# Where the softmax shift is split into two bf16 parts: in VectorE after the maxima, or behind TensorE's transpose

## The reference

```python
x = x + L0_attn(layernorm(x))                    # 16 heads of width 8, 4 key/value heads
x = x + L0_xattn(layernorm(x), ctx, ctx)         # 16 heads of width 8
x = x + L0_ffn(layernorm(x))                     # 8 experts, 2 chosen, 1 shared
x = x + L1_attn(layernorm(x))                    # shared heads, relative bias
x = x + L1_xattn(layernorm(x), ctx, ctx, mask)   # 16 heads of width 8
x = x + L1_ffn(layernorm(x))

# the attention of the two 16-head forms, for each batch and head
scores = Q @ K.T / sqrt(8)
attn = softmax(scores)          # exp(scores - max) / sum
out = attn @ V
```

## Time and profile before

| | |
|---|---|
| time, median of 3 runs | 1096.98 us (1094.63 to 1103.36) |
| profiled execution, its span from first to last instruction | 1087.7 us |
| the median less that span | 9.3 us |
| busy share of the span: PE, PEld, DVE, ACT, POOL | 89%, 64%, 79%, 64%, 60% |
| chain that ended last | PE 61%, DVE 19%, issue 8%, DMA 5%, ACT 3%, POOL 3% |
| steps of the stage heads | about 31 to 355 us of the span |
| steps of the stage cross1 | about 736 to 920 us |

### The profile page before, as it was taken

The page is one execution under the profiler, slowest core; times in us unless marked ns, Lnnn a source line. Parts: engine busy times, 40 slices in busy tenths (PEclk is TensorE's granted clock), DMA queues, the critical chain, the costliest instruction groups (busy, mean ns, idle before and its releaser), DMA issues.

```text
span 1087.7 us, 33962 instructions
## 1 busy us (share of the span) xinstructions
PE 973.1 (89%) x10494; PEld 694.1 (64%) x10494; DVE 855.0 (79%) x2398; ACT 692.1 (64%) x1801; POOL 649.3 (60%) x1020
## 2 busy tenths in 40 slices
PE   3699999989998888999998889889999999768997
PEld 2466666656665667777776677665656655556885
DVE  6588899888888778888887888776787877657665
ACT  1377777777776743555665887673666666546775
POOL 8757778877676466640675786168667752323443
PEclk9599999999998979999998999998999999989999
DMA  5776567985666201332332111035555640054551
GB/s 147 181 148 132 116 139 163 185 162 134 143 153 171 74 34 50 98 105 77 106 104 55 37 31 38 26 64 133 115 113 129 130 106 18 6 196 167 194 193 29
DMA packets 81460, 119.69 MB, mean 110 GB/s; under 512 B 16720, under 2 KB 62704, under 8 KB 80288
## 3 DMA queue, kind: packets, MB, share of 16 engines
q1 hardware_dynamic: 66704, 85.24, 32.9%
q0 software_dynamic: 9472, 27.27, 8.2%
q10 hardware_dynamic: 5136, 5.31, 2.5%
HBM read 80.75 MB, written 36.18 MB: 107 GB/s over the span
## 4 chain that ended last, share of the span: by engine, by line
PE 61%; DVE 19%; issue 8%; DMA 5%; ACT 3%; POOL 3%; SPq 1%; DVEq 0%; POOLq 0%; ACTq 0%
PE heads_ps_pv L992 4%; PE heads_ps_max L970 4%; DVE heads_neg_max L770 4%; PE cross_ps_max L960 4%; PE experts_ps_gu L2488 4%; PE cross_ps_max L970 3%; PE cross_ps_pv L992 3%; DMA QK<-heads_qk_parts 2%; PE experts_ps_gu L2490 2%; PE experts_ps_gu L2489 2%; PE heads_ps_out L1054 2%; PE experts_ps_y L2509 2%; PE experts_ps_y L2510 2%; PE experts_ps_hT L2496 1%; PE cross_ps_qk L1316 1%
## 5 line engine op out<-in xcount | busy, mean ns | idle before, releaser
L770 DVE TENSOR_REDUCE heads_neg_max<-heads_ps_max 128x4 f32<-128x512 f32 x256 | 169.5, 681 | 36.0 <-PE heads_ps_max L970 34.4
L844 ACT ACTIVATE heads_E<-heads_ps_exp 128x512 f32<-128x512 f32 x256 | 150.1, 603 | 22.1 <-PE heads_ps_pv L992 17.3
L970 PE MATMUL heads_ps_max<-QK 48*128 48x128 bf16 x1024 | 102.9, 226 | 10.2 <-DMA QK<-heads_qk_parts 5.8
L770 DVE TENSOR_REDUCE cross_neg_max<-cross_ps_max 128x4 f32<-128x512 f32 x128 | 86.2, 682 | 29.5 <-PE cross_ps_max L970 28.9
L974 PE MATMUL heads_ps_exp<-QK 50*128 50x128 bf16 x1024 | 103.0, 222 | 0.0
L2182 POOL DMA_INDIRECT experts_gathered<-experts_y_dram,experts_index x64 | 62.0, 969 | 65.4 <-DMA experts_y_dram<-experts_y_sb 44.1
L844 ACT ACTIVATE cross_E<-cross_ps_exp 128x512 f32<-128x512 f32 x128 | 76.5, 599 | 33.1 <-PE cross_ps_exp L974 17.0
L2404 ACT ACTIVATE experts_act_out<-experts_ps_gu 128x256 f32<-128x256 f32 x110 | 42.3, 384 | 83.0 <-PE experts_ps_gu L2490 82.9
L970 PEld LDWEIGHTS heads_ps_max<-QK 48*128 48x128 bf16 x1024 | 58.9, 97 | 52.2 <-issue 21.0
L1613 POOL TENSOR_TENSOR experts_hidden_lo<-experts_hidden,experts_hidden_hi 128x512 fp32r<-128x512 f32 x32 | 41.4, 1293 | 73.9 <-ACT experts_hidden_hi L1837 66.8
L992 PE MATMUL heads_ps_pv<-heads_E,heads_V 128*32 128x128 f32 x2048 | 84.8, 285 | 0.0
(11 more groups left out here) (325 smaller groups left out, 3173.3 us busy)
## 6 DMA issues: line engine op xcount, KB each, us to landing
experts_share<-experts_cT_dram SPq DMA_DIRECT2D x7, 2304.0 KB, 8.8
heads_qk_parts<-heads_parts POOLq DMA_DIRECT2D x32, 384.0 KB, 4.7
QK<-heads_qk_parts SPq DMA_DIRECT2D x64, 192.0 KB
QK<-heads_qk_parts SPq DMA_DIRECT2D x64, 128.0 KB
cross_qk_parts<-cross_parts POOLq DMA_DIRECT2D x16, 384.0 KB, 4.2
QK<-cross_qk_parts SPq DMA_DIRECT2D x32, 192.0 KB
experts_xs_dram<-load_stats SPq DMA_DIRECT2D x26, 192.0 KB, 3.0
experts_xs<-experts_xs_dram SPq DMA_DIRECT2D x78, 64.0 KB
```

What stands on the lines that cost most here:

```text
L770: nc.vector.tensor_reduce(neg_max[:, half, heads.start:heads.stop], ps_max[:, u % 2, :].rearrange("q (h k) -> q h k", h=HU), AX.X, ALU.max ...
L844: nc.scalar.activation(E[:, half, heads.start:heads.stop, :], ps_exp[:, u % 2, :].rearrange("k (h q) -> k h q", h=HU), ACT.Exp, scale=scal ...
L970: last_max = nc.tensor.matmul(ps_max[:, u % 2, i * S:(i + 1) * S], QK[q_of][rows, 0, h, max_of], QK[q_of][rows, 1, h, max_of], start=not m ...
```

## The change

VectorE no longer makes `shift` after the fourth maximum. TensorE transposes the 16 columns of fp32 negative maxima (now in two buffers) into 16 fp32 rows of PSUM, as soon as the fourth maximum is taken. ScalarE's copy from PSUM, still L856's place, writes the high part in bf16; a new VectorE subtraction (`shift_low`, behind the output's addition L784 and ahead of the third maximum) takes PSUM less the high part and writes the low part. It, no longer the copy, raises `shiftT_ready`, for which SyncE (ahead of L606), `project_qk` and the next `turn_shift` wait. SyncE's two DMAs now take one part each for both halves, instead of both parts of one half each; each still moves 16 rows of 128 bf16. The second set of semaphores (`shift_ready`) goes.

```diff
@@ -446,9 +446,8 @@
         rest = sb("rest", [D, GT])
         parts = [sb(f"parts{p}", [D, 2, PARTS, GT], BF16) for p in range(2)]
         V = [sb(f"V{p}", [S, G, H * TILE + SLOT]) for p in range(RING)]
-        neg_max = sb("neg_max", [S, HALVES, HH])
-        shift = sb("shift", [S, HALVES, SHIFT, HH], BF16)
-        shiftT = [sb(f"shiftT{p}", [SHIFT * H, S], BF16) for p in range(2)]
+        neg_max = [sb(f"neg_max{p}", [S, HALVES, HH]) for p in range(2)]
+        shiftT = [sb(f"shiftT{p}", [H, SHIFT, S], BF16) for p in range(2)]
         E = sb("E", [S, HALVES, HH, S])
         recip = sb("recip", [S, H])
         oT_spread = sb("oT_spread", [D, 2, S])
@@ -456,7 +455,7 @@
         oT = sb("oT", [D, S])
         qk_dram = [nc.dram_tensor(f"{name}_qk_parts{p}", (2, PARTS, D, GT), BF16) for p in range(RING)]
 
-        ps_shiftT = ps_qk[0:SHIFT * H, 0, 0:S // 2].bitcast(BF16)
+        ps_shiftT = ps_qk[0:H, 0, 0:S]
         o_spread = ps_pv[:, 0:2 * S].rearrange("q (h d) -> q h d", d=SLOT)
 
         masked = mask is not None
@@ -492,7 +491,6 @@
         max_scored = sem("max_scored")
         max_taken = sem("max_taken")
         shift_hi = sem("shift_hi")
-        shift_ready = sem("shift_ready")
         shiftT_made = sem("shiftT_made")
         shiftT_ready = sem("shiftT_ready")
         shift_placed = [sem(f"shift_placed{p}") for p in range(2)]
@@ -601,9 +599,9 @@
                     turned = shiftT[(t.k + MA - 1) % 2]
                     sp.wait_ge(shiftT_ready, t.batch(1, MA))
                     apart(sp, t, turns_sp)
-                    for half in range(HALVES):
-                        at = half * BASE + ROWS
-                        sp.dma_start(QK[p][at:at + SHIFT, 0, :, j * S:j * S + S], turned[half * SHIFT * HH:(half + 1) * SHIFT * HH, :]).then_inc(shift_placed[(t.k + MA - 1) % 2], 16)
+                    for i in range(SHIFT):
+                        at = ROWS + i
+                        sp.dma_start(QK[p][at:at + BASE + 1:BASE, 0, :, j * S:j * S + S], turned[:, i, :]).then_inc(shift_placed[(t.k + MA - 1) % 2], 16)
                 if t.has(-2 * LA, 2 * NG_ALL - 1 - 2 * LA):
 
                     p, half = slot(t, LA), t.k % 2
@@ -765,10 +763,17 @@
                 if t.has(-MA, NB_ALL - MA - 1):
                     dve.wait_ge(max_scored, t.batch(UNITS, MA * UNITS + u + 1))
                     if u == 0:
-                        need(dve, shift_ready, t.batch(1, MA))
+                        need(dve, shiftT_made, t.batch(1, MA - 1))
                     half, heads = heads_of(u)
-                    nc.vector.tensor_reduce(neg_max[:, half, heads.start:heads.stop], ps_max[:, u % 2, :].rearrange("q (h k) -> q h k", h=HU),
+                    nc.vector.tensor_reduce(neg_max[(t.k + MA) % 2][:, half, heads.start:heads.stop], ps_max[:, u % 2, :].rearrange("q (h k) -> q h k", h=HU),
                                             AX.X, ALU.max, negate=True).then_inc(max_taken, 1)
+
+            def shift_low(t):
+
+                if t.has(1 - MA, NB_ALL - MA):
+                    turned = shiftT[(t.k + MA - 1) % 2]
+                    dve.wait_ge(shift_hi, t.batch(1, MA))
+                    nc.vector.tensor_tensor(turned[:, 1, :], ps_shiftT, turned[:, 0, :], ALU.subtract).then_inc(shiftT_ready, 1)
 
             def emit(t):
                 odd = t.k % 2 == 1
@@ -782,6 +787,7 @@
                     dve.wait_ge(x_biased, t.group(1, 0))
                     xb = row(x_sb, t.batch(1, -2 - layer_at(t, -2) * B))
                     nc.vector.tensor_tensor(xb, ps_out[:, 1, :], xb, ALU.add).then_inc(x_done, 1)
+                shift_low(t)
                 maxima(t, 2)
                 if t.has(1, NB_ALL):
 
@@ -791,13 +797,6 @@
                     need(dve, oT_made, t.batch(1, -1))
                     nc.vector.tensor_tensor(o_tok[:], o_spread[:, :, 0:HD], recip[:].unsqueeze(2).to_broadcast([S, H, HD]), ALU.mult).then_inc(o_ready, 1)
                 maxima(t, 3)
-                if t.has(-MA, NB_ALL - MA - 1):
-
-                    dve.wait_ge(max_taken, t.batch(UNITS, (MA + 1) * UNITS))
-                    need(dve, shiftT_made, t.batch(1, MA))
-                    nc.vector.tensor_copy(shift[:, :, 0, :], neg_max[:]).then_inc(shift_hi, 1)
-                    dve.wait_ge(shift_hi, t.batch(1, MA + 1))
-                    nc.vector.tensor_tensor(shift[:, :, 1, :], neg_max[:], shift[:, :, 0, :], ALU.subtract).then_inc(shift_ready, 1)
                 if t.has(2, NB_ALL + 1):
                     dve.wait_ge(x_done, t.batch(1, -1))
                     apart(dve, t, turns_dve)
@@ -853,7 +852,7 @@
                     q = (t.k + MA - 1) % 2
                     act.wait_ge(shiftT_made, t.batch(1, MA))
                     need(act, shift_placed[q], t.group(32, 32))
-                    nc.scalar.copy(shiftT[q][:], ps_shiftT).then_inc(shiftT_ready, 1)
+                    nc.scalar.copy(shiftT[q][:, 0, :], ps_shiftT).then_inc(shift_hi, 1)
                 if prev:
                     act.wait_ge(pv_done, t.batch(UNITS, 0))
                     need(act, spread_turned, t.batch(1, -1))
@@ -1028,11 +1027,11 @@
 
             def turn_shift(t):
 
-                pe.wait_ge(shift_ready, t.batch(1, MA))
+                pe.wait_ge(max_taken, t.batch(UNITS, MA * UNITS))
                 need(pe, shiftT_ready, t.batch(1, MA - 1))
                 qk = t.group(2, 2 * FA)
                 need(pe, qk_ready, min(2 * NG_ALL, qk) if t.reg is None else qk)
-                nc.tensor.transpose(ps_shiftT, shift[:].rearrange("q a i h -> q (a i h)"), identb[:]).then_inc(shiftT_made, 1)
+                nc.tensor.transpose(ps_shiftT, neg_max[(t.k + MA - 1) % 2][:].rearrange("q a h -> q (a h)"), ident[:]).then_inc(shiftT_made, 1)
 
             def turn_spread(t):
```

## The result

The kernel after took 1114.84 us (median of 4 executions, 1108.13 to 1124.21) against 1095.81 of before beside it: a ratio of 1.0178, 95% interval 1.0127 to 1.0229. The sign and the mechanism of the prediction held; the size did not, as the loss is about 19 to 28 us and not 9.5: the first set lies near the upper end of the range on record (1089 to 1117 us), the second above it. The profiled execution was the slowest of the first four, with a span of 1122.3 us; that of before had 1087.7. The profiles of e4_before_held and e7_bf16_maxima were taken in disturbed executions, so of these only the lists of waits, stretches at full clock and, once, the place of a fall of the clock are read.

A forecast was written before the change was run, and what follows sets the result against it. It took the SyncE loop, with the QK loads queued behind the later shift, to bind heads after the change: +8.5 us there, +1.0 in cross1, +9.5 on 1096.98, so 1106.5 us, range 1089 to 1117.

The forecast's parts named there:

- L1035's wait goes: In heads, `turn_shift` no longer waits for VectorE's L800; these waits were counted as 32.8 us in 62.
- the second rival: The engines win: the compute loop decides in heads, 1085 us; chance 0.12.
- The shift is ready 1.3 us later than the copy: Odd steps of heads: shift ready at about +3.15, L606 at +3.2, first L621 at +4.5 us.
- shift later still: Rival: ScalarE's casts or VectorE's order hold the subtraction 0.4 us more, +11 on top, 1117 us; chance 0.14.
- The subtraction costs 0.29 us: New VectorE subtraction takes 0.29 us like L784, bounds 0.17 and 0.74, never stretched by GpSimd.
- The landing: Heads, first L621 to the half's landing: 5.8 us to 161 us, 6.0 to 201, 7.5 to 233, 5.3 to 323.
- The 0.05 us from the landing to the scores: SyncE loop in heads: 0.05 us added to the period between the QK load's landing and the scores.
- The estimate of 2.3 us: Skill page's landing time for a 128 KB DMA; set aside for the trace's 4.0 to 4.7 us on SyncE's queue.
- Half of the third stretch: Heads, 201 to 233 us: 3 pairs x 1.35 = +4.1 us, of which half was counted, +2.0.
- The loops cancel: Rival: later transfers meet less traffic, each half lands 0.3 us sooner, -8 us, 1098 us; chance 0.24.
- The engines win: Rival: halves land within 4.8 us of their first L621, pairs in heads take 9.4 us, 1085 us; chance 0.12.
- The fp32 transposition costs 0.075 us: TensorE's fp32 transpose against bf16: +0.075 us, bounds 0 and 0.31; cross1 taken as +1, bounds 0 and 2.4.

The follow-up runs named there:

- the second: The kernel after, unchanged, executed again beside the kernel before: 1122.47 us, ratio 1.0266.
- e4_before_held: The kernel before, with one wait added on SyncE ahead of L606, for VectorE's addition to x (L784) of the same step: 1117.58 us, 1.0188.
- e7_bf16_maxima: The kernel after with bf16 maxima and a bf16 transposition, so the low part is zero: 1100.82 us, 1.0054.
- e3_low_early: The kernel after with the new subtraction moved between the first and second maximum in VectorE's order: 1093.24 us, 1.0012.
- e1_load_first: The kernel after with SyncE's three loads of QK put ahead of the shift's wait and DMAs in every step: 1099.84 us, 1.0077.
- e10_two_queues: e3_low_early with the high part's DMA issued on ScalarE's queue, leaving one issue ahead of the loads: 1091.06 us, 0.9975.
- e5_odd_loads_first: The kernel after with SyncE's three loads of QK ahead of the shift's wait and DMAs in odd steps only: 1102.7 us, 1.0083.

## Why the prediction was right in its course and short in its size

- *L1035's wait goes*: right, 11.2 us in 27 waits of the matmul became 2.6 in 2, and 21.6 us in 35 of the weight load 4.7 in 6. The 32.8 us in 62 waits of the prediction count time twice: in 25 of the waits both rows show the same idle time. The sum did not use this figure; the second rival did.
- *The shift is ready 1.3 us later than the copy*: forecast +3.15, measured +3.02; L604 at +3.05 (forecast +3.2); the first load at +4.16 here and at +4.55, +4.16, +5.16 and +4.51 on the mean of the four stretches (forecast +4.5), as the two issues now take 1.07 us and not 1.28. e3_low_early and e4_before_held show that this delay by itself gives and takes the loss. The rival *shift later still* falls, though the time of the first set lies in its band.
- *The subtraction costs 0.29 us*: 0.27, and never stretched: 268 to 270 ns in 96 of them, where L800 went from 174 to 745. The Trainium skill (SBUF — State Buffer, Who interferes with whom) has it that a VectorE instruction with at most one SBUF input, outside the 2-port modes, does not contend with GpSimd; this row agrees, and 61 of the 96 lay beside an operation of GpSimd.
- *The landing.* From the first load to the landing the means are 5.7, 6.35, 6.6 and 5.7 us; I took 5.8, 6.0, 7.5 and 5.3. The fourth was mis-sized: the nearest row, the 4.0 us median of ctx in that stretch, was too far a relative: it is one DMA of 128 KB, a half of QK is three of 192, 128 and 64 KB, issued within 0.9 us of each other (that their sum sets the landing was not tested). The term of -0.8 became +3.8, which holds the stretch's one fall of the clock as well. Of the 0.51 us by which a pair of that stretch passed the forecast, 0.36 are the landing.
- *The 0.05 us from the landing to the scores*: the other 0.14 of that 0.51. Steps written out have 0.05 us (183.06 + 5.70 = 188.76, scores at 188.81); where the reading step is in the hardware loop, it is 0.23 or more:

```profile
305.07 5.18 DMA QK<-heads_qk_parts
310.25 0.23 issue
310.48 0.21 PE heads_ps_max L969
```

That is some 0.18 us in 16 of the 27 pairs, 3 us of the 9 by which the pairs of heads passed the forecast.

- *The estimate of 2.3 us* for 128 KB, worked out from the Trainium skill (DMA: Bandwidth & Descriptors, Anatomy of one DMA), is for a DMA that GpSimd issues; on SyncE's queue the third loads of these odd steps, 64 KB behind 320, took 4.0 to 6.4 us to land, the one in the chain above 5.70.
- *Half of the third stretch*: the transfers there do land sooner than the 7.5 us of before (6.6), as the halving meant, but the pairs took 12.42 us and not the 11.37 of the halved term: the first loads started at +5.16 and not +4.5, and 13 us of the stretch ran at 1.2 GHz. That the clock is the reason was not tested.
- *The loops cancel*: its 0.3 us a half did not come; only the third stretch shows it. *The engines win*: it needed a landing within 4.85 us; of the 29 odd steps one had that (4.84). The engines' own pair was 9.57 us in e1_load_first, 0.17 over my 9.4, and 9.33 in e3_low_early and e10_two_queues, in pairs whose loads were in time. The fp32 transposition is the same in all three; what parts them is a wait that the sum did not have, of `project_qk` (L1014) for the late subtraction: 2.8 us in 12 weight loads (0.23 each) in e1_load_first, none in the other two.
- *The fp32 transposition costs 0.075 us*: 0.175, by e7_bf16_maxima. For cross1 that is 16 x 0.35 = 5.6 us where I took +1 with 2.4 as the upper bound. The profile shows only +1.8, because before itself lost 2.3 us more in its second and third pairs (10.90 and 11.97 us against 9.26 and 11.32), at a lower clock (0.98 against 1.00 in that stage).
- *What was not in the sum*: the clock. The step "what is late next" ended at the scores and did not ask what granted clock TensorE works at while and after it waits. In the profiled execution the 14.8 us behind step 59, and part of the third and fourth stretch, go with that; e4_before_held's pairs at full clock show that the late loads cost 0.2 to 0.4 us a pair by themselves, 27 x 0.3 = 8 us, which is what I had forecast for them. How the rest of the 19 to 28 us of the medians parts between the clock and the fp32 transposition (at most 96 x 0.175 = 17 us, where TensorE is the bound; 5.6 of them in cross1) the runs don't tell.

## What to carry to other kernels

Work that is taken off a busy engine can come back as latency on a queue that the busy table doesn't list: before moving a producer, follow what its semaphore releases, with every DMA issued behind that wait, to the reader. An instruction that depends on a short chain should stand in its engine's order ahead of one that waits for another engine; moving one line (e3_low_early) gave the whole loss back. The slack of the reader sets the price: before, the loads landed 0.9 us ahead of the scores on the mean, and 1.0 to 1.4 us of delay (2.1 in the third stretch) used that up.

## What the runs showed of the hardware that I had not expected

- The landing of a load follows its issue only in part: in the fourth stretch starts at +4.51, +3.15, +2.60 and +1.84 (after, e3_low_early, e10_two_queues, e5_odd_loads_first) landed at +10.17, +9.29, +9.23 and +9.43. The loads of two steps share one queue, which would explain it; no run separated them.
- A transposition of 16 columns in fp32 costs TensorE 0.175 us more than in bf16, of which its own row shows 0.06; some 0.12 lie ahead of it, at its weight load (e7_bf16_maxima).
- From a landing to the matmul that waits for it there are 0.05 us in steps written out and 0.23, at times 0.32, in steps of the hardware loop, as a rule, in every kernel here whose loads came last.
- Waits of TensorE's matmuls for the loads, 0.2 to 2.9 us in 18 of the 30 odd steps from step 1 on, go with stretches at 1.2 GHz that cost more than the wait: the pair that starts at 210.06, behind a wait of 1.50 us, took 12.25 us. That the wait brings the fall is not shown.
